# Beta, scatter halves and scatter order in the second attention stage of a two-layer kernel

## The chip, the cores and the metric

The kernel runs on one core of a Trainium2 chip, as one program. The metric is device time in microseconds of one execution. Three runs of the kernel before took 1773.91, 1776.12 and 1784.85 us; the median, 1776.12, stands for it. One more execution was profiled, and the rows below are from it.

## The reference

Two layers act on x, 64 x 64 tokens of 256 numbers (T = 4096 rows). Each layer is a cross attention and then a mixture of experts, both with a residual and a layer norm in front. What the change touches is in the second layer (and, for the scatter, in the first layer's experts too):

```python
x = x + _L0_xattn_ref(_layernorm(x), ctx, ...)
x = x + _L0_ffn_ref(_layernorm(x), ...)       # 16 experts, top 2, and a shared expert
x = x + _L1_xattn_ref(_layernorm(x), ctx, mask, ...)
x = x + _L1_ffn_ref(_layernorm(x), ...)       # 32 experts, top 4

# the end of _L1_xattn_ref
delta = rs * (ctx @ Wo.T + bo)
mu, var = delta.mean(-1), ((delta - mu) ** 2).mean(-1)
delta = (delta - mu) / sqrt(var + EPS_LN) * ln_gamma + ln_beta
# the routing of _L1_ffn_ref
topk_logits, topk_idx = top_k(x @ gate_w.T + gate_b, 4)
topk_weight = softmax(topk_logits)
y = sum over the 4 chosen experts of topk_weight * expert(x)
```

## The kernel before

The kernel is written by hand for the five engines; every wait is a semaphore written in the code, and each engine runs its own list of instructions in order. The 4096 rows are 32 tiles of 128 (NT); four tiles are a group (GT = 4, NG = 8). The stages follow one another: attention one (to 770 us of the span), the shared expert with the first routing (to 910), the experts of layer one (to 1050), attention two with the second routing (to 1425), the experts of layer two (to 1700), and a stage that adds the experts' rows up by token.

Attention two (`attention1`, line 1477) runs a software pipeline of steps r = 0, 1, 2, ... on each engine. In step r TensorE makes the scores of tile r + 1, the output of tile r and the projection of tile r - 1. VectorE's step (line 1903) clips the scores of tile r + 1, finishes the residual of tile r - 2 (`residual`, line 1892), normalises the heads of tile r and takes the mean and variance of the projected tile r - 1 (`delta_statistics`). At fixed places in a group's four steps it also does the layer norms in front of attention and experts (`norm_statistics` and `norm_apply`, lines 1437 to 1470: `apply_a` is the attention's, `apply_f` the experts') and the routing: `choose` picks four experts a token, `place_rows` gives each row its slot, `weigh` its weights.

GpSimd's step (line 1984) does for VectorE what VectorE hands it: `delta_deviation` (line 1978) raises the variance of tile r - 2 to the power -1/2; `add_beta` (line 1972) makes xb = x + beta for tile r - 1, which `residual` waits for; `deviation` (line 1969; the instruction is at 1456) does the power of a group's four variances. Early in the stage it also adds up the first layer's expert rows (lines 1964 and 1967). From step 10 on (FIRST) it runs one scatter round a step: `Routing.scatter` (line 1164) sends the four tiles of one group to the slots of their k-th expert. A round writes place (an integer) and weight into the tail of each row of xf, two copies, then issues four indirect DMAs of 128 rows of 1088 bytes. The same rows of xf are sent four times with different tails, so a round with k > 0 first waits until all four DMAs of the group's round before have landed (`scattered`). There are 32 rounds: the first 22 run in plain order (group by group, k = 0 to 3); the last ten are interleaved between groups 5, 6 and 7 by a list (lines 1573 to 1575):

```python
in_order = [(q, k) for q in range(NG) for k in range(m.K)][:NT - FIRST]
rounds = in_order + [(NG - 3, 2), (NG - 2, 0), (NG - 3, 3), (NG - 2, 1), (NG - 1, 0), (NG - 2, 2), (NG - 1, 1),
                     (NG - 2, 3), (NG - 1, 2), (NG - 1, 3)]
```

In step 33 GpSimd does the power of the last group (`last_group`) ahead of its scatter round. The four slot tables form a ring (RING = 4); `mark_sent` waits until a group's DMAs have all landed.

SyncE loads the second layer's weights into the room that attention two leaves, in 16 pieces of 512 KB (line 1609). Each load waits for a count of `tails_set`, so that the pieces go out with the last rounds, two a round; the last two wait for the round of index 29. After that SyncE writes the zero padding behind the experts' rows (`table_pads`, line 714; the DMAs are at line 726; ScalarE writes the other half), waits for all padding, and loads the first rows of the expert stage (lines 855 and 863), which also waits for GpSimd's last rounds to land.

The shared expert's stage calls the same `scatter` for its 16 rounds, with k = 0 and 1.

Of the kernel before, what the change touches and what calls it, by code (L numbers as in the profile page):

```python
# [4 lines left out]
F32 = mybir.dt.float32  # L5
BF16 = mybir.dt.bfloat16
I32 = mybir.dt.int32
# [4 lines left out]
P = 128  # L12
B, S, H = 64, 64, 256
T = B * S
NT = T // P
# [509 lines left out]
class Moe:  # L525
# [17 lines left out]
    def tables(self, ctx, nc, views=None):  # L543
# [5 lines left out]
        self.place = sbt("_place", [P, NG, K, GT], I32)  # L549
        self.weight = sbt("_weight", [P, NG, K, GT], F32)  # L550
# [22 lines left out]
class Constants:  # L573
# [6 lines left out]
    def tables(self, pool):  # L580
# [13 lines left out]
        for m in moes:  # L594
# [4 lines left out]
            nc.gpsimd.iota(m.place[:, :, :, :], pattern=[[GT * P * m.K, NG], [1, m.K], [P * m.K, GT]], base=0,  # L599
                           channel_multiplier=m.K).then_inc(made, 1)  # L600
            nc.gpsimd.memset(m.total[:, :], 0.0).then_inc(made, 1)
        nc.gpsimd.iota(sb["zeros"][:, DEST:DEST + 1].bitcast(I32), pattern=[[0, 1]], base=DUMP,
                       channel_multiplier=1).then_inc(made, 1)
# [177 lines left out]
def experts(stages, block, nc, sb, m, w_gu, w_down, bias, entered):  # L781
# [133 lines left out]
    def _(act):  # L915
# [3 lines left out]
        def step(it, r):  # L919
            if exists(it, r + 2):  # L920
# [4 lines left out]
                if q >= TAILS:  # L925
                    act.wait_ge(rows_stored[q % OUTS], 32 * ((q - TAILS) // OUTS + 1))
                nc.scalar.activation(dest[:, q % TAILS, :].bitcast(I32),
                                     rows[:, q % BODY, :, DEST].bitcast(I32), ACT.Copy)
# [94 lines left out]
class Routing:  # L1023
# [3 lines left out]
    def __init__(self, ph, nc, sb, m, wg, bias):  # L1027
# [24 lines left out]
        self.scattered = [ph.sem(f"scattered{n}") for n in range(Routing.RING)]  # L1052
# [64 lines left out]
    def weigh(self, dve, it, q, done):  # L1117
# [8 lines left out]
        nc.vector.tensor_tensor(m.weight[:, bass.ds(it * 2 + q, 1), :, :].rearrange("p a k j -> p (a j) k"), self.powers[:, :, :],  # L1126
# [37 lines left out]
    def scatter(self, pool, it, q, xn, k, turn, done):  # L1164

        m, nc = self.m, self.nc
        sent = 16 * GT
        slot, lap = (it * 2 + q) % self.RING, (it * 2 + q) // self.RING
        if k == 0:
            done(pool, self.slots_ready, it, q)  # L1170
            done(pool, self.weights_ready, it, q)
        else:
            pool.wait_ge(self.scattered[slot], lap * sent * m.K + sent * k)
        nc.gpsimd.tensor_copy(xn[:, :, DEST].bitcast(I32), m.place[:, it * 2 + q, k, :])
        nc.gpsimd.tensor_copy(xn[:, :, WEIGHT], m.weight[:, it * 2 + q, k, :]).then_inc(self.tails_set, 1)
        pool.wait_ge(self.tails_set, turn + 1)
        for j in range(GT):
            n = j * m.K + k
            pool.indirect_dma_start(m.rows_in, bass.IndirectOffsetOnAxis(ap=self.slots[:, slot, n:n + 1], axis=0),  # L1179
                                    xn[:, j, :], None).then_inc(self.scattered[slot], 16)  # L1180
# [5 lines left out]
    def mark_sent(self, pool, it, q):  # L1186

        n = 16 * GT * self.m.K
        slot, lap = (it * 2 + q) % self.RING, (it * 2 + q) // self.RING
        pool.wait_ge(self.scattered[slot], n * (lap + 1))  # L1190
# [1146 lines left out]
```

## Time and profile before

| | us |
|---|---|
| median of 3 runs (lowest, highest) | 1776.12 (1773.91, 1784.85) |
| the profiled execution, its own time | 1775.95 |
| its span in the profile | 1774.0 |
| busy in the span: TensorE, VectorE, ScalarE, GpSimd | 1533.0, 1332.5, 1094.1, 1093.0 |

The profile shows one execution: for each engine what instruction ran when, by the line of the kernel that issued it, how long the engine was idle before it and what ended that idle time. PE is TensorE, DVE is VectorE, ACT is ScalarE, POOL is GpSimd, SP is SyncE, and SPq is SyncE's queue. Times in rows are microseconds from the span's start, unless marked ns.

### The profile page before, as it was taken

To read this page: it belongs to the slowest core of one execution; us is meant where nothing else is said; L and a number is where in the kernel's file an instruction comes from. 1 tells how busy PE (TensorE), PEld (TensorE's weight loads), DVE (VectorE), ACT (ScalarE), POOL (GpSimd) and SP (SyncE) were. 2 spreads that over 40 slices of the span, in tenths; PEclk is the share of its full clock that TensorE was granted. 3 is DMA by queue.
4 is the path that set the end of the run, shared out by engine and by line. 5 is a ranking of instruction groups with operands and counts; after the bars stand their busy time and mean duration, and the time that the engine had idled before them with its cause. 6 is when DMAs were issued, how large, how long until landed. Compare 5 with 4: busy or idle time off the path is not lost.

```text
span 1774.0 us, 43982 instructions
## 1 busy us (share of the span) xinstructions
PE 1533.0 (86%) x14968; PEld 1236.6 (70%) x14968; DVE 1332.5 (75%) x2901; ACT 1094.1 (62%) x3516; POOL 1093.0 (62%) x1111
## 2 busy tenths in 40 slices
PE   6999999999999999989967755998895179999966
PEld 5888888888888888866646642565564179998955
DVE  6889899899999989876634344798886248887876
ACT  5888888888888888843335433656551056666610
POOL 4767667676666667647635554647776636666642
PEclk9999999999999999989989986999995589999988
DMA  8400000000000000022255424112213855554456
GB/s 230 128 20 20 20 20 20 20 20 20 12 19 20 20 20 20 8 97 84 79 176 155 151 80 161 49 38 94 83 71 113 311 167 165 162 158 150 125 200 275
DMA packets 103082, 167.66 MB, mean 95 GB/s; under 512 B 20224, under 2 KB 75981, under 8 KB 102481
## 3 DMA queue, kind: packets, MB, share of 16 engines
q1 hardware_dynamic: 73984, 103.46, 19.1%
q0 software_dynamic: 22272, 56.15, 8.6%
q10 hardware_dynamic: 6608, 5.25, 1.0%
q8 instruction: 124, 2.03, 0.5%
q14 instruction: 94, 0.76, 0.2%
HBM read 95.31 MB, written 75.76 MB: 96 GB/s over the span
## 4 chain that ended last, share of the span: by engine, by line
PE 68%; DVE 11%; issue 9%; POOL 3%; another core or an unknown queue 3%; ACT 2%; ACTq 1%; DMA 1%; SPq 1%; DVEq 0%; POOLq 0%
PE layers_banks L323 13%; PE layers_banks L294 13%; PE layers_banks L309 9%; PE layers_banks L890 9%; PE layers_banks L901 5%; PE layers_banks L1269 3%; PE layers_banks L277 3%; PE layers_banks L283 3%; PE layers_banks L878 2%; DVE weights L1862 2%; PE layers_banks L1282 1%; PE layers_banks L2152 1%; POOL l_rows_in L1179 1%; PE layers_banks L1071 1%
## 5 line engine op out<-in xcount | busy, mean ns | idle before, releaser
L468 POOL TENSOR_TENSOR w_down<-w_down,layers_arena 128x1024 f32<-128x1024 f32 x256 | 483.5, 1894 | 230.3 <-DVE layers_arena L424 229.3
L389 ACT ACTIVATE w_down<-layers_banks,layers_arena 128x256 f32<-128x256 f32 x1024 | 468.7, 498 | 2.8 <-DVE layers_arena L418 2.8
L1010 POOL DMA_INDIRECT l_by_token<-layers_arena x240 | 245.0, 1021 | 192.3 <-issue 104.2
L429 DVE COPY w_down<-layers_banks 128x1024 f32<-128x1024 f32 x256 | 312.2, 1220 | 40.4 <-PE layers_banks L309 36.2
L418 DVE TENSOR_REDUCE layers_arena<-layers_banks 128x4 f32<-128x1024 f32 x256 | 309.4, 1209 | 29.4 <-PE layers_banks L294 29.3
L294 PE MATMUL layers_banks<-layers_arena 64*128 64x256 f32 x2048 | 277.9, 383 | 3.7 <-ACT w_down L389 2.2
L323 PE MATMUL layers_banks<-w_down,layers_arena 128*64 128x256 f32 x2048 | 249.4, 385 | 1.7 <-DVE w_down L429 1.3
L389 ACT ACTIVATION_READ_ACCUMULATOR w_down<-layers_banks,layers_arena 128x1 f32 x1024 | 238.0, 232 | 0.0
L890 PE MATMUL layers_banks<-layers_arena 128*128 128x128 f32 x1600 | 204.1, 280 | 34.3 <-ACT layers_arena L933 30.7
L1179 POOL DMA_INDIRECT l_rows_in<-layers_arena,l_routing_group_slots x192 | 190.3, 991 | 57.7 <-issue 44.7
L309 PEld LDWEIGHTS layers_banks<-ident,w_down 64*128 64x128 f32 x4096 | 168.4, 138 | 77.5 <-issue 71.6
L890 PEld LDWEIGHTS layers_banks<-layers_arena 128*128 128x128 f32 x1600 | 192.3, 195 | 40.4 <-issue 40.0
L294 PEld LDWEIGHTS layers_banks<-layers_arena 64*128 64x128 f32 x2048 | 208.7, 188 | 6.0 <-issue 5.5
L309 PE MATMUL layers_banks<-ident,w_down 64*128 64x64 f32 x4096 | 178.7, 224 | 17.4 <-DVE w_down L429 3.4
L323 PEld LDWEIGHTS layers_banks<-w_down,layers_arena 128*64 128x64 f32 x2048 | 142.1, 136 | 61.5 <-DVE w_down L429 1.5
L986 DVE TENSOR_SCALAR layers_arena<-layers_banks,layers_arena 128x256 f32<-128x256 f32 x240 | 104.5, 477 | 75.5 <-PE layers_banks L901 41.0
L924 ACT ACTIVATE layers_arena<-layers_banks 128x512 f32<-128x512 f32 x120 | 70.5, 587 | 92.8 <-PE layers_banks L878 78.2
L353 ACT ACTIVATE layers_arena<-layers_banks 128x512 f32<-128x512 f32 x128 | 75.8, 592 | 82.0 <-PE layers_banks L283 82.0
L933 ACT ACTIVATE layers_arena<-weights 128x512 f32 (+1 forms) x240 | 119.6, 547 | 3.7 <-issue 3.7
L957 DVE TENSOR_SCALAR layers_arena<-layers_banks,l_block_bias 128x128 f32<-128x128 f32 x160 | 48.8, 346 | 87.1 <-PE layers_banks L890 84.7
L878 PE MATMUL layers_banks<-ident,layers_arena 128*128 128x128 f32 x480 | 75.4, 281 | 44.0 <-DMA layers_arena<-l_rows_in 44.0
L878 PEld LDWEIGHTS layers_banks<-ident,layers_arena 128*128 128x128 f32 x480 | 61.9, 146 | 57.0 <-issue 44.1
(227 smaller groups left out, 2552.3 us busy)
## 6 DMA issues: line engine op xcount, KB each, us to landing
layers_arena<-l_rows_in SPq DMA_DIRECT2D x240, 136.0 KB
weights<-l_by_token SPq DMA_DIRECT2D x32, 512.0 KB, 9.7
layers_arena<-in_ctx SPq DMA_DIRECT2D x64, 128.0 KB, 2.7
layers_arena<-l_by_token SPq DMA_DIRECT2D x32, 256.0 KB, 2.7
weights<-in_w_gu SPq DMA_DIRECT2D x16, 512.0 KB
l_rows_in<-zeros SPq DMA_DIRECT2D x1, 4352.0 KB
x_sb<-in_x SPq DMA_DIRECT2D x32, 128.0 KB, 2.5
w_down<-in_w_down SPq DMA_DIRECT2D x1, 4096.0 KB
```

The source lines that it names most:

```text
L294: last = nc.tensor.matmul(ps_s[:, b, 2 * h + qt, :], q_sb[half, p % 2, b, qt * P:(qt + 1) * P], ctx_d[half, p // TILE % 2, b, :], start=Tr ...
L309: last = nc.tensor.transpose(ps_t[:, d, kt, c * S:(c + 1) * S], prob[half, n % 4, c, kt * P:(kt + 1) * P], ident[half, half])
L323: last = nc.tensor.matmul(ps_qo[b * S:(b + 1) * S, 0, 0:A_N], vb[:, p // TILE % 2, kt, b, head * S:(head + 1) * S], prob_t[:, p % 2, b, kt ...
L389: last = nc.scalar.activation(prob[:, n % 4, c, :], ps_s[:, n % 2, c, :], ACT.Exp, bias=negmax[:, n % 2, c:c + 1], accum_out=sums[:, n % 2 ...
L418: nc.vector.tensor_reduce(negmax[:, n % 2, :], ps_s[:, n % 2, :, :], AX.X, ALU.max, negate=True).then_inc(max_ready, 1)
L429: nc.vector.tensor_copy(prob_t[:, n // 2 % 2, n % 2, :, :, :].rearrange("p k c (d s) -> p d (k c) s", d=2), ps_t[:, :, :, :].rearrange("p ...
L468: nc.gpsimd.tensor_tensor(prob[:, n % 4, :, :], prob[:, n % 4, :, :], rsum[:, n % 2, :].unsqueeze(2).to_broadcast([P, 4, A_N]), ALU.mult). ...
L878: last = nc.tensor.transpose(ps_x[:, q % 2, b, kt, :], rows[:, q % BODY, b, kt * P:(kt + 1) * P], sb["ident"][:, :])
L890: last = nc.tensor.matmul(ps_gu[:, q % 2, u, b, :], w_now[:, q % 2, b, kt, u * P:(u + 1) * P], rows_t[:, q % 2, b, kt, :], start=(kt == 0) ...
L933: last = nc.scalar.activation(w_now[:, r % 2, b, :, :].rearrange("p k n -> p (k n)"), w_gu[:, bass.ds(e[b], 1), :, :].rearrange("p a k n - ...
L1010: pool.indirect_dma_start(m.by_token, bass.IndirectOffsetOnAxis(ap=place, axis=0), outs[:, r % OUTS, b, :], None, bounds_check=T * m.K - 1 ...
L1179: pool.indirect_dma_start(m.rows_in, bass.IndirectOffsetOnAxis(ap=self.slots[:, slot, n:n + 1], axis=0), xn[:, j, :], None).then_inc(self. ...
```

## The change

Five things change. (1) `add_beta` goes from GpSimd to VectorE: `residual` makes xb itself, ahead of its wait for the power. (2) Place and weight lie side by side as two floats in one table, `tails`, instead of an integer table and a float table; what reads the place converts it to an integer. (3) A scatter round is two halves of two tiles: each half waits only for its own two DMAs of the group's round before, with a semaphore of its own, sets place and weight with one copy, and sends its two tiles. `tails_set` counts halves, and SyncE's thresholds double. (4) All 32 rounds run in plain order. (5) In step 33 the last group's power stands ahead of the fourth DMA of that step's round instead of ahead of the round.

```diff
-        self.place = sbt("_place", [P, NG, K, GT], I32)
-        self.weight = sbt("_weight", [P, NG, K, GT], F32)
+        self.tails = sbt("_tails", [P, NG, K, GT, 2], F32)
...
                 nc.scalar.activation(dest[:, q % TAILS, :].bitcast(I32),
-                                     rows[:, q % BODY, :, DEST].bitcast(I32), ACT.Copy)
+                                     rows[:, q % BODY, :, DEST], ACT.Copy)
...
-        self.scattered = [ph.sem(f"scattered{n}") for n in range(Routing.RING)]
+        self.scattered = [[ph.sem(f"scattered{n}_{half}") for half in range(2)] for n in range(Routing.RING)]
...
-    def scatter(self, pool, it, q, xn, k, turn, done):
+    def scatter(self, pool, it, q, xn, k, turn, done, ahead_of_last=None):
 
         m, nc = self.m, self.nc
-        sent = 16 * GT
+        sent = 16 * (GT // 2)
         slot, lap = (it * 2 + q) % self.RING, (it * 2 + q) // self.RING
         if k == 0:
             done(pool, self.slots_ready, it, q)
             done(pool, self.weights_ready, it, q)
-        else:
-            pool.wait_ge(self.scattered[slot], lap * sent * m.K + sent * k)
-        nc.gpsimd.tensor_copy(xn[:, :, DEST].bitcast(I32), m.place[:, it * 2 + q, k, :])
-        nc.gpsimd.tensor_copy(xn[:, :, WEIGHT], m.weight[:, it * 2 + q, k, :]).then_inc(self.tails_set, 1)
-        pool.wait_ge(self.tails_set, turn + 1)
-        for j in range(GT):
-            n = j * m.K + k
-            pool.indirect_dma_start(m.rows_in, bass.IndirectOffsetOnAxis(ap=self.slots[:, slot, n:n + 1], axis=0),
-                                    xn[:, j, :], None).then_inc(self.scattered[slot], 16)
+        for half in range(2):
+            tiles = slice(half * GT // 2, (half + 1) * GT // 2)
+            if k > 0:
+                pool.wait_ge(self.scattered[slot][half], lap * sent * m.K + sent * k)
+            nc.gpsimd.tensor_copy(xn[:, tiles, DEST:WEIGHT + 1], m.tails[:, it * 2 + q, k, tiles, :]).then_inc(self.tails_set, 1)
+            pool.wait_ge(self.tails_set, 2 * turn + half + 1)
+            for j in range(half * GT // 2, (half + 1) * GT // 2):
+                n = j * m.K + k
+                if j == GT - 1 and ahead_of_last is not None:
+                    ahead_of_last()
+                pool.indirect_dma_start(m.rows_in, bass.IndirectOffsetOnAxis(ap=self.slots[:, slot, n:n + 1], axis=0),
+                                        xn[:, j, :], None).then_inc(self.scattered[slot][half], 16)
...
-    in_order = [(q, k) for q in range(NG) for k in range(m.K)][:NT - FIRST]
-    rounds = in_order + [(NG - 3, 2), (NG - 2, 0), (NG - 3, 3), (NG - 2, 1), (NG - 1, 0), (NG - 2, 2), (NG - 1, 1),
-                         (NG - 2, 3), (NG - 1, 2), (NG - 1, 3)]
+    rounds = [(q, k) for q in range(NG) for k in range(m.K)]
+    IN_LOOP = NT - FIRST
...
-            sp.wait_ge(rt.tails_set, len(in_order) + 1 + n * (len(rounds) - len(in_order) - 2) // len(later))
+            sp.wait_ge(rt.tails_set, 2 * (IN_LOOP + 1 + n * (len(rounds) - IN_LOOP - 2) // len(later)))
...
         def residual(it, r):
             tile = x_sb[:, bass.ds(it * BODY + r, 1), :].rearrange("p a n -> p (a n)")
+            tdone(dve, x_ready, it, r - 1)
+            nc.vector.tensor_tensor(xb[:, r % 2, :], tile, w["beta"][:, :], ALU.add).then_inc(xb_ready, 1)
             tdone(dve, rstd_d_ready, it, r)
-            tdone(dve, xb_ready, it, r)
-            tdone(dve, x_ready, it, r - 1)
             nc.vector.scalar_tensor_tensor(out=scaled[:, :], in0=delta[:, r % 2, :], scalar=mv_d[:, r % 2, 0:1],
                                            in1=w["gamma"][:, :], op0=ALU.subtract, op1=ALU.mult).then_inc(scaled_ready, 1)
             tdone(dve, scaled_ready, it, r)
+            tdone(dve, xb_ready, it, r)
             nc.vector.scalar_tensor_tensor(out=tile, in0=scaled[:, :], scalar=rstd_d[:, r % 2:r % 2 + 1],
                                            in1=xb[:, r % 2, :], op0=ALU.mult, op1=ALU.add).then_inc(x_ready, 1)
...
-        def add_beta(it, r):
-            tdone(pool, scaled_ready, it, r - 2)
-            tdone(pool, x_ready, it, r - 2)
-            nc.gpsimd.tensor_tensor(xb[:, r % 2, :], x_sb[:, bass.ds(it * BODY + r, 1), :].rearrange("p a n -> p (a n)"),
-                                    w["beta"][:, :], ALU.add).then_inc(xb_ready, 1)
...
-            if texists(it, r - 1):
-                add_beta(it, r - 1)
...
             last_group = j == 1 and g == NG
+            ahead = None
             if last_group:
-                deviation(it, g - 1, vare_f, rstd_f, steps_f, xf_ready, rstd_f_ready)
+                def ahead():
+                    deviation(it, g - 1, vare_f, rstd_f, steps_f, xf_ready, rstd_f_ready)
             if 0 <= r - FIRST < len(rounds):
                 q, k = rounds[r - FIRST]
-                rt.scatter(pool, it, q, xf[:, q % XF, :, :], k, r - FIRST, gdone)
+                rt.scatter(pool, it, q, xf[:, q % XF, :, :], k, r - FIRST, gdone, ahead)
```

The parts left out fill `tails` and its readers in the same way (the iota of the places, the sigmoids and the weights of the routings, the last stage's weights) and wait for both halves in `mark_sent`.

## Rows read from the trace of the kernel before

**Rows 1.** Busy time by stretch: busy us (instructions) per engine, clock, DMA share.

```profile
core 0: us, PE busy (x) PEld busy (x) DVE busy (x) ACT busy (x) POOL busy (x), PEclk, DMA share, GB/s
770.00:910.00 140.00, 119.17 (x636) 79.67 (x632) 83.48 (x361) 42.87 (x76) 79.77 (x107) 0.95 0.30 111
1240.00:1273.00 33.00, 29.88 (x298) 19.59 (x296) 28.72 (x91) 19.28 (x33) 25.03 (x35) 1.00 0.26 86
1334.00:1368.00 34.00, 19.46 (x138) 14.48 (x136) 26.44 (x91) 4.70 (x7) 22.60 (x30) 0.50 0.28 97
1368.00:1426.00 58.00, 9.29 (x50) 7.14 (x50) 11.05 (x47) 1.24 (x2) 38.88 (x55) 0.50 0.83 290
```

**Rows 2.** Chain that ended last, in the loop: start us, us, what.

```profile
1240.56 1.31 DVE layers_arena L1441 x4
...
1266.19 1.40 another core or an unknown queue
...
1273.38 1.31 DVE layers_arena L1441 x4
```

**Rows 3.** Chain that ended last, at the stage's end, SyncE's part.

```profile
1403.90 0.33 SPq L1609
...
1423.26 1.93 DMA l_rows_in<-zeros
```

**Rows 4.** Timeline of GpSimd at the stage's end: start, us, then idle before and releaser.

```profile
1368.17 1.01 POOL L1456 TENSOR_TENSOR layers_arena<-layers_arena,minus_half 128x4 f32<-128x4 f32 x1 [4.21 <-DVE layers_arena L1449]
...
1387.27 0.19 POOL L1174 COPY layers_arena<-l_place 128x4 int32<-128x4 int32 x1 [1.70 <-DVE l_weight L1126]
...
1392.78 0.21 POOL L1174 COPY layers_arena<-l_place 128x4 int32<-128x4 int32 x1
1392.90 0.20 POOL L1175 COPY layers_arena<-l_weight 128x4 f32<-128x4 f32 x1
1393.38 0.98 POOL L1179 DMA_INDIRECT l_rows_in<-layers_arena,l_routing_group_slots  x1 [0.28 <-issue]
...
1398.16 0.20 POOL L1174 COPY layers_arena<-l_place 128x4 int32<-128x4 int32 x1
...
1416.89 0.19 POOL L1174 COPY layers_arena<-l_place 128x4 int32<-128x4 int32 x1 [2.58 <-DMA l_rows_in<-layers_arena,l_routing_group_slots]
...
1421.29 0.96 POOL L1179 DMA_INDIRECT l_rows_in<-layers_arena,l_routing_group_slots  x1 [0.30 <-issue]
```

**Rows 5.** Groups of GpSimd, 1060 to 1430: busy us, mean ns, idle before.

```profile
L1975 POOL TENSOR_TENSOR layers_arena<-x_sb,w_beta 128x256 f32<-128x256 f32 x32 | 23.9, 747 | 0.0
...
L1174 POOL COPY layers_arena<-l_place 128x4 int32<-128x4 int32 x32 | 8.4, 261 | 14.1 <-DMA l_rows_in<-layers_arena,l_routing_group_slots 12.3 <-DVE l_weight L1126 1.7
```

**Rows 6.** Timeline of VectorE, two independent adds one after the other.

```profile
1062.42 0.42 DVE L1848 TENSOR_TENSOR x_sb<-x_sb,layers_arena 128x256 f32<-128x256 f32 x1
1062.77 0.42 DVE L1846 TENSOR_TENSOR layers_arena<-layers_arena 128x256 f32<-128x256 f32 x1
```

**Rows 7.** Timeline of VectorE: residual and apply instructions, stretched and not.

```profile
1141.67 0.94 DVE L1897 SCALAR_TENSOR_TENSOR layers_arena<-layers_arena,w_gamma 128x256 f32<-128x256 f32 x1 [2.81 <-POOL layers_arena L1981]
...
1214.33 0.48 DVE L1897 SCALAR_TENSOR_TENSOR layers_arena<-layers_arena,w_gamma 128x256 f32<-128x256 f32 x1
...
1215.88 1.42 DVE L1465 TENSOR_SCALAR layers_arena<-x_sb,layers_arena 128x256 f32<-128x256 f32 x4
...
1218.95 1.79 DVE L1465 TENSOR_SCALAR layers_arena<-x_sb,layers_arena 128x256 f32<-128x256 f32 x4 [0.17 <-POOL layers_arena L1456]
```

**Rows 8.** Timeline of VectorE: its waits in steps 26, 27 and 31.

```profile
1314.87 0.42 DVE L1880 TENSOR_TENSOR layers_arena<-layers_banks,w_bo 128x256 f32<-128x256 f32 x1 [0.76 <-PE layers_banks L1687]
...
1317.81 1.23 DVE L1862 TENSOR_SCALAR weights<-layers_banks 128x1024 f32<-128x1024 f32 x1 [1.37 <-PE layers_banks L1650]
...
1349.51 0.95 DVE L1897 SCALAR_TENSOR_TENSOR layers_arena<-layers_arena,w_gamma 128x256 f32<-128x256 f32 x1 [1.91 <-issue]
```

**Rows 9.** Timeline of GpSimd: three of the beta adds.

```profile
1126.34 0.73 POOL L1975 TENSOR_TENSOR layers_arena<-x_sb,w_beta 128x256 f32<-128x256 f32 x1
...
1133.75 0.72 POOL L1975 TENSOR_TENSOR layers_arena<-x_sb,w_beta 128x256 f32<-128x256 f32 x1
...
1219.40 0.87 POOL L1975 TENSOR_TENSOR layers_arena<-x_sb,w_beta 128x256 f32<-128x256 f32 x1
```

**Rows 10.** Groups of the page: one of ScalarE in the expert stages.

```profile
L924 ACT ACTIVATE layers_arena<-layers_banks 128x512 f32<-128x512 f32 x120 | 70.5, 587 | 92.8 <-PE layers_banks L878 78.2
```

More of the change, by code:

```diff
@@ L598, in tables @@
                            allow_small_or_imprecise_dtypes=True).then_inc(made, 1)
-            nc.gpsimd.iota(m.place[:, :, :, :], pattern=[[GT * P * m.K, NG], [1, m.K], [P * m.K, GT]], base=0,
-                           channel_multiplier=m.K).then_inc(made, 1)
+            nc.gpsimd.iota(m.tails[:, :, :, :, 0], pattern=[[GT * P * m.K, NG], [1, m.K], [P * m.K, GT]], base=0,
+                           channel_multiplier=m.K, allow_small_or_imprecise_dtypes=True).then_inc(made, 1)
             nc.gpsimd.memset(m.total[:, :], 0.0).then_inc(made, 1)
-        nc.gpsimd.iota(sb["zeros"][:, DEST:DEST + 1].bitcast(I32), pattern=[[0, 1]], base=DUMP,
-                       channel_multiplier=1).then_inc(made, 1)
+        nc.gpsimd.iota(sb["zeros"][:, DEST:DEST + 1], pattern=[[0, 1]], base=DUMP,
+                       channel_multiplier=1, allow_small_or_imprecise_dtypes=True).then_inc(made, 1)
     def tables_made(self, eng):
@@ L1125, in weigh @@
         dve.sem_inc(self.passed, 1)
-        nc.vector.tensor_tensor(m.weight[:, bass.ds(it * 2 + q, 1), :, :].rearrange("p a k j -> p (a j) k"), self.powers[:, :, :],
+        nc.vector.tensor_tensor(m.tails[:, it * 2 + q, :, :, 1].rearrange("p k j -> p j k"), self.powers[:, :, :],
                                 self.share[:, 1, :].unsqueeze(2).to_broadcast([P, GT, m.K]), ALU.mult)\
@@ L1186, in mark_sent @@
     def mark_sent(self, pool, it, q):
-        n = 16 * GT * self.m.K
+        n = 16 * (GT // 2) * self.m.K
         slot, lap = (it * 2 + q) % self.RING, (it * 2 + q) // self.RING
-        pool.wait_ge(self.scattered[slot], n * (lap + 1))
+        for half in range(2):
+            pool.wait_ge(self.scattered[slot][half], n * (lap + 1))
         pool.sem_inc(self.rows_sent, 1)
@@ L1335, in sigmoids @@
             done(act, rt.behind_ready, it, q)
-            nc.scalar.activation(m.weight[:, bass.ds(it * 2 + q, 1), 0, :], rt.behind[:, :, 1].unsqueeze(1), ACT.Sigmoid,
+            nc.scalar.activation(m.tails[:, it * 2 + q, 0, :, 1], rt.behind[:, :, 1], ACT.Sigmoid,
                                  scale=-1.0)
-            nc.scalar.activation(m.weight[:, bass.ds(it * 2 + q, 1), 1, :], rt.behind[:, :, 1].unsqueeze(1), ACT.Sigmoid)\
+            nc.scalar.activation(m.tails[:, it * 2 + q, 1, :, 1], rt.behind[:, :, 1], ACT.Sigmoid)\
                 .then_inc(rt.weights_ready, 1)
@@ L2180, in expert_weights @@
             nc.vector.tensor_tensor(weighted[:, :, :, :], onehot[:, :, :, :],
-                                    m.weight[:, g, :, :].rearrange("p k j -> p j k").unsqueeze(3)
+                                    m.tails[:, g, :, :, 1].rearrange("p k j -> p j k").unsqueeze(3)
                                     .to_broadcast([P, GT, K, E]), ALU.mult).then_inc(expert_steps, 1)
```

## The prediction

> **What bounds the kernel now.** I read the page's chain and groups first, then the busy times by stretch, then the chain and the timelines of VectorE, GpSimd and SyncE inside attention two. All edits but the scatter's own lie in attention two, 1060 to 1425 us of the span. The stretches [rows 1] show TensorE 29.9 and VectorE 28.7 us busy of 33 in the middle of its loop, and TensorE 19.5 of 34, at half clock, at its end; from 1368 on only GpSimd, issuing indirect DMAs, and the DMA engines are busy. In the loop the chain of waits is VectorE nearly throughout: four tiles take 1273.38 - 1240.56 = 32.8 us, broken by waits on "another core or an unknown queue" [rows 2]. There are four such between 1150 and 1308, 1.4 to 1.8 us each; the row shows the third. TensorE, just behind, is the second limit. GpSimd keeps pace; what it does shows only where VectorE waits for it.
>
> The end is another matter. After VectorE's last statistics GpSimd runs nine scatter rounds, and SyncE may issue the last weight loads only when the round of index 29 has its tails set; it then writes 16 blocks of padding, the last of which ends the stage [rows 3]. Two chains therefore end almost together: GpSimd's last DMA issue ends at 1421.29 + 0.96 = 1422.3 [rows 4] and still has to land, and SyncE's padding lands at 1425.2 [rows 3]. SyncE's is the later.
>
> **Beta on VectorE.** GpSimd loses 32 adds of 0.75 us [rows 5]; VectorE gets 32 of 128x256 f32 from SBUF. A like add takes 0.42, but the next independent one starts 1062.77 - 1062.42 = 0.35 later [rows 6]; in residual() nothing depends on the add until after the next instruction, so I take 0.35 a tile. The bounds: 0 where VectorE would have waited anyhow; at most 0.35 + (0.94 - 0.48) = 0.81, if the add is stretched as L1897 is where a GpSimd tensor op runs beside it [rows 7]. I stay with 0.35, since GpSimd's tensor op of that size is the one that goes.
>
> The Trainium skill, "VectorE: DVE Perf Modes", section on the DRAIN, says that the next instruction does not start until the pipe is empty. That would make the add cost its whole 0.42, and the sum 1.5 us more; the rows show 0.35.
>
> Which of the 32 lie on the path? Tiles 0 to 3: VectorE waits for GpSimd or TensorE there (2.8 us at tile 3 [rows 7]), so hidden. Tiles 25 and 26: it waits 0.76 and 1.37 for TensorE [rows 8], hidden. Tile 29: it waits 1.91 for GpSimd's power, behind a scatter round [rows 8], hidden. That leaves 25. Four of these stand right before the waits on an unknown queue [rows 2], whose end VectorE does not set, so they are swallowed. So 21 x 0.35 = +7.4 us.
>
> Taken off: from 1118 to 1141 the chain is GpSimd itself, adding up expert rows, with two beta adds of 0.7 between them [rows 9]: -1.4. L1897 at 1141.67 would also get back 0.46, but the two new VectorE adds there run beside GpSimd's tensor ops and stretch those; I let these cancel. In five groups the four instructions of apply_a take 1.79 instead of 1.42, each time with a beta add beside them (the row at 1219.40 stands inside the one at 1218.95) [rows 7, 9]: 5 x 0.37 = -1.9. The loop thus gives 7.4 - 1.4 - 1.9 = +4.1: the last statistics come 4.1 us later.
>
> **Half rounds.** A round now takes 1398.16 - 1392.78 = 5.38, of which 0.60 pass before its first DMA [rows 4]; the four DMAs and three gaps of 0.30 are 4.78. One copy instead of two saves 0.12 before the first DMA, and a second copy and wait, 0.48, takes the place of one gap of 0.30: 4.78 - 0.30 + 2 x 0.48 = 5.44. So half rounds cost +0.06 each, but a half waits only for its own two DMAs of the round before, with 2.7 us of the other half between. In the loop the landing waits are 12.3 us in all [rows 5], hidden behind VectorE; removing them brings nothing. The shared expert also runs scatter(), but TensorE has 119 busy of 140 us there [rows 1] and is its chain: 0. Place as a float, read by ScalarE with a conversion, and weights at stride two keep the number of instructions and of elements; in the expert stage ScalarE sits 92.8 us idle before L924 alone [rows 10]: 0, and if 240 such small copies grew by a tenth of a microsecond, still under that cover.
>
> **Plain order and the power between.** Before, GpSimd is idle 4.2 us before the last group's power at 1368.17, 1.7 before group 7's first round and 2.6 for a landing before the last one [rows 4]. After, three DMAs of round 23 fill the first idle time; then come the power (1.0), one DMA, and eight rounds: 1368.2 + 1.0 + 1.0 + 8 x 5.44 = 1413.7, before the shift of 4.1. Group 7's first round would begin at 1370.2 + 4 x 5.44 = 1392, after its weights (1387.3), so the 1.7 goes. GpSimd's chain gains 8.5.
>
> SyncE's does not. Its gate is the second half of round 29: 1370.2 + 5 x 5.44 + 2.9 = 1400.3, against 1403.9 [rows 3]: -3.6 at best. Rounds 28 to 31 are now all of group 7, in the stretch where the DMA engines are 83% busy [rows 1], and I must bound the landing: 2.6 us after the last issue (the wait at 1416.89) as the lower end; as the upper, 5.4, since the round at 1398.16 does not wait for the one whose DMAs ended at 1392.78 [rows 4]. Two halves hide 2.7, so round 29 waits 0 to 2.7 and the gate gains 3.6 to 0.9. I take the middle, -2.3; what SyncE does after the gate, 21.3 us, stays. The later GpSimd rounds, with up to three such waits, end at 1413.7 to 1421.8 and stay about level with SyncE.
>
> Sum: +4.1 - 2.3 = +1.8 us. Against the profiled execution, 1775.95 us (span 1774.0 and 1.95 around it), that is 1777.8; the median of the three runs is 0.2 higher: 1778.
>
> **Rivals.**
> - *The adds are free*: VectorE's new 0.35 vanishes in TensorE's time. For: TensorE is almost as full, and the waits on an unknown queue [rows 2] are not VectorE's. Against: between 1150 and 1200 VectorE waits for nobody. Then -1.4 - 1.9 - 2.3 = -5.6: 1770.5.
> - *The padding is not the end*: with the loads issued earlier, SyncE's padding finds its queue empty and GpSimd's -8.5 counts in full: 4.1 - 8.5 = -4.4, 1771.7. Against: the loads move with the rounds, so the padding meets the same queue.
> - *The added operand blocks*: slower. Each new add, with two inputs in SBUF, is stretched by 0.46 as L1897 was, and 21 x 0.81 = 17.0 instead of 7.4: +11.4, 1787.5. For: that row [rows 7]. Against: L1897 at 1214.33 takes 0.48 while an indirect DMA is being issued. It decides from 0.27 us a tile, where the adds eat all three gains (5.6/21). The Trainium skill, "SBUF — State Buffer", section "SBUF: two separate sides", has this rule: a VectorE instruction with two SBUF inputs and a GpSimd instruction that reads SBUF exclude each other for the whole instruction. The trace agrees for L1897 beside L1975; for the small tail copies no row shows it.
> - *The clock falls in the loop*: TensorE, waiting more, drops to half clock before 1334, as it does there now. One group at half clock adds about 29.9 us of TensorE time less 3 us of slack: 1805. Against: full clock in the loop's stretches [rows 1].
>
> **How the numbers follow.** The forecast 0.50, free adds 0.20, padding 0.10, blocked adds 0.12, clock 0.05, something else 0.03. The landing bounds move the forecast by 1.4 either way, the runs themselves by several. From 1770.5 less that spread to 1787.5 plus it gives 1767 to 1789. One per cent, 17.8 us, is about what can be told from no change: faster than 1758 only by something unseen, 0.03; slower than 1794 by the clock or a mishap, 0.06; within, 0.91.
>
> **What would show it.** Right: 32 new VectorE adds of about 0.42; four tiles of the loop in about 34 us; the 1.79 of apply_a back at 1.42; no GpSimd idle time before the last power; landing waits near 3 us instead of 12; 21 us between SyncE's last load and the first expert rows. Wrong: four tiles still in 32.8, or new adds of 0.8, or padding that ends well after or before GpSimd's last landing.

## The result, and the profile after

The changed kernel took 1806.37 us (median of 4 runs, 1801.14 to 1810.43) against 1775.17 us for the kernel before (4 runs beside it). The ratio of their runs is 1.0146, with a 95% interval from 1.0115 to 1.0177. The two medians are 31.2 us apart; by the ratio the change costs about 26 us. The forecast was 1778, +1.8, with 1767 to 1789 as its range. The profiled execution of the changed kernel took 1801.14 us with a span of 1799.3, so the two profiled executions are 25.3 us apart in their spans.

Where these 25.3 us lie follows from the starts of a few instructions in both traces: the first routing logits of the shared expert's stage, the experts' first row load (SyncE), the first `add_parts` and the first and last clip of attention two (VectorE), the last logits (TensorE), and the row loads again.

| stretch, us | before | after | difference |
|---|---|---|---|
| to the first logits | 783.9 | 782.2 | -1.7 |
| shared expert: first logits to first row load | 124.9 | 141.8 | **+16.9** |
| first experts, to the first add_parts | 153.2 | 152.3 | -0.9 |
| to the first clip | 38.4 | 38.4 | 0 |
| attention two's loop: first to last clip | 241.5 | 254.0 | **+12.5** |
| last clip to last logits | 35.1 | 36.3 | +1.2 |
| tail: last logits to first row load | 49.0 | 48.3 | -0.7 |
| first to last row load of the second experts | 244.8 | 241.9 | -2.9 |
| the rest | 103.2 | 104.1 | +0.9 |

Two stretches hold the loss: one in which the forecast had 0, and one in which it had +4.1. Stretches with the same code differ between executions: the shared stage of kernels that do not touch it lies between 124 and 128.5, the second experts' between 240 and 251, and two kernels below with the same loop (e4 and e7) have it at 243.4 and 238.1. A difference of 5 us between two loops, each from one execution, is therefore not told from none; the two losses above are well beyond that.

**The shared expert's stage.** Busy times of the whole stretch, after and then before; the columns are those of [rows 1].

```profile
782.00:924.00 142.00, 122.68 (x560) 78.64 (x560) 73.26 (x333) 41.31 (x71) 76.58 (x103) 0.90 0.27 102
```

```profile
784.00:909.00 125.00, 111.99 (x560) 74.86 (x560) 73.51 (x333) 40.95 (x70) 74.20 (x102) 0.96 0.30 113
```

TensorE runs the same 560 matmuls, 10.7 us longer busy at a lower granted clock; VectorE does no more than before, GpSimd 2.4 us more. The group of TensorE that grew is the gate and up product. After, then before (busy us, mean ns of one, idle before it):

```profile
L1272 PE MATMUL layers_banks<-layers_arena,weights 128*128 128x512 f32 x128 | 69.0, 699 | 11.8 <-DVE x_sb L1396 8.2 <-issue 3.7
```

```profile
L1269 PE MATMUL layers_banks<-layers_arena,weights 128*128 128x512 f32 x128 | 58.4, 607 | 4.4 <-DVE x_sb L1393 3.6 <-issue 0.7
```

Busy +10.6 and idle +7.4 make 18.0, no less than the whole stretch's 16.9. One group shows how. TensorE before: down product, gate and up of the next group, down again.

```profile
828.59 3.63 PE L1282 MATMUL layers_banks<-weights,layers_arena 128*128 128x256 f32 x16
...
833.28 7.11 PE L1269 MATMUL layers_banks<-layers_arena,weights 128*128 128x512 f32 x16 [0.73 <-DVE x_sb L1393]
...
842.83 3.63 PE L1282 MATMUL layers_banks<-weights,layers_arena 128*128 128x256 f32 x16
```

VectorE before, the residual that follows the down product: the first pair of tiles needs its first eight matmuls, the second pair the other eight.

```profile
830.71 0.86 DVE L1393 SCALAR_TENSOR_TENSOR x_sb<-layers_banks,layers_arena,x_sb 128x256 f32<-128x256 f32 x2
832.25 0.88 DVE L1393 SCALAR_TENSOR_TENSOR x_sb<-layers_banks,layers_arena,x_sb 128x256 f32<-128x256 f32 x2 [0.68 <-PE layers_banks L1282]
```

TensorE after, and VectorE after:

```profile
848.41 3.63 PE L1285 MATMUL layers_banks<-weights,layers_arena 128*128 128x256 f32 x16
...
854.45 8.80 PE L1272 MATMUL layers_banks<-layers_arena,weights 128*128 128x512 f32 x16 [2.08 <-DVE x_sb L1396]
...
865.70 3.63 PE L1285 MATMUL layers_banks<-weights,layers_arena 128*128 128x256 f32 x16
```

```profile
852.64 1.66 DVE L1396 SCALAR_TENSOR_TENSOR x_sb<-layers_banks,layers_arena,x_sb 128x256 f32<-128x256 f32 x4 [2.35 <-remote]
```

The down product takes 3.63 us in both. Before, VectorE starts on the first pair 2.1 us after its beginning. After, it starts 4.2 us after it, and then does all four tiles at once. "remote" means that a semaphore moved at that moment, but no instruction in the profile ends near it: by the record of its rows TensorE was through with these eight matmuls some 2.3 us earlier. I call this a late handover. The next gate and up product, which needs the same bank, begins 854.45 - 848.41 = 6.04 us after the down product instead of 4.69 (+1.35), and takes 8.80 instead of 7.11 (+1.69), since TensorE, after 2.08 us idle, is granted half its clock (0.50, the 1.2 GHz level) soon after it has resumed:

```profile
854.00:856.00 2.00, 1.55 (x3) 0.82 (x4) 1.85 (x9) 0.00 (x0) 0.00 (x0) 0.82 0.00 0
856.00:858.00 2.00, 2.00 (x3) 0.67 (x2) 1.86 (x12) 0.00 (x0) 1.38 (x2) 0.50 0.00 0
```

Together 3.04 us a group: the period is 17.29 (865.70 - 848.41) instead of 14.24 (842.83 - 828.59). On GpSimd the difference is the landing wait, which is there before (first fence) and gone after (second):

```profile
845.62 0.19 POOL L1174 COPY layers_arena<-weights 128x4 int32<-128x4 int32 x1 [2.93 <-DMA l_rows_in<-layers_arena,l_routing_group_slots]
```

```profile
846.03 0.19 POOL L1175 COPY layers_arena<-weights 128x4 f32<-128x4 f32 x1
```

**The loop.** VectorE's waits over 20 tiles in the middle, before and after:

```profile
DVE layers_arena L1082 <- remote: 3.6, 2, 1.8
DVE weights L1862 <- remote: 2.5, 2, 1.2
DVE layers_arena L1880 <- PE layers_banks L1687: 0.8, 1, 0.8
```

```profile
DVE layers_arena L1871 <- remote: 11.7, 9, 2.2
DVE weights L1864 <- PE layers_banks L1652: 2.6, 4, 1.0
DVE layers_arena L1081 <- remote: 1.4, 2, 0.7
```

```profile
1168.90:1342.60 173.70, 151.42 (x1449) 98.24 (x1446) 142.97 (x453) 93.73 (x154) 97.14 (x132) 0.96 0.20 68
```

The last row is the same 20 tiles after, 173.7 us; before they took 161.0 with VectorE 138.45 busy:

```profile
1156.80:1317.80 161.00, 144.62 (x1437) 94.82 (x1436) 138.45 (x433) 92.71 (x154) 109.95 (x151) 1.00 0.22 74
```

Of the +12.7, VectorE's work is 4.5, late handovers 13.1 - 6.1 = 7.0. Most are now at L1871, where VectorE takes up TensorE's product of weights and values (I call it P·V). VectorE's new adds are as forecast from [rows 6], and the apply instructions are no longer stretched as in [rows 7]:

```profile
L1468 DVE TENSOR_SCALAR layers_arena<-x_sb,layers_arena 128x256 f32<-128x256 f32 x37 | 13.0, 412 | 0.0
...
L1897 DVE TENSOR_TENSOR layers_arena<-x_sb,w_beta 128x256 f32<-128x256 f32 x20 | 8.4, 419 | 0.0
```

**The tail.** GpSimd's landing waits at the end, from 1395 on, where before the row at 1416.89 in [rows 4] had the only long one; and SyncE's timeline, whose end answers to [rows 3]:

```profile
POOL layers_arena L1175 <- DMA l_rows_in<-layers_arena,l_routing_group_slots: 8.0, 5, 2.9
```

```profile
1384.94 51.36 SPq L1611 DMA_DIRECT2D weights<-in_w_gu  x16
1437.03 12.07 SPq L725 DMA_DIRECT2D l_rows_in<-zeros  x16
```

SyncE's last padding is issued by 1449.1. GpSimd's last scatter issue runs to 1450.59, and the row loads start at 1453.3. So GpSimd's chain, not SyncE's, now ends the stage.

### The profile page after: what moved, and what is told of

Read it like the earlier page. It is cut to its first block and busy times, and to the rows that moved or that the text cites. A ratio compares the mean times of both kernels' runs of the same rounds, so it can differ in the third digit from the quotient of the medians.

```text
span 1799.3 us, 43952 instructions
## 1 busy us (share of the span) xinstructions
PE 1552.0 (86%) x14968; PEld 1248.4 (69%) x14968; DVE 1340.5 (74%) x2933; ACT 1094.4 (61%) x3516; POOL 1078.0 (60%) x1079
## 5 line engine op out<-in xcount | busy, mean ns | idle before, releaser
L889 PE MATMUL layers_banks<-layers_arena 128*128 128x128 f32 x1600 | 208.2, 283 | 28.4 <-ACT layers_arena L932 23.4
## 6 DMA issues: line engine op xcount, KB each, us to landing
layers_arena<-in_ctx SPq DMA_DIRECT2D x64, 128.0 KB, 2.7
x_sb<-in_x SPq DMA_DIRECT2D x32, 128.0 KB, 2.5
```

Source lines behind the costliest of these rows:

```text
L889: last = nc.tensor.matmul(ps_gu[:, q % 2, u, b, :], w_now[:, q % 2, b, kt, u * P:(u + 1) * P], rows_t[:, q % 2, b, kt, :], start=(kt == 0) ...
```

## The experiments

Times stand as medians with the ratio to the kernel before on the same chip; the lengths of stretches are each from one profiled execution, by the marks of the table above.

**Landing waits put back, in both scatter stages** (e1):

```diff
+        if k > 0:
+            for half in range(2):
+                pool.wait_ge(self.scattered[slot][half], lap * sent * m.K + sent * k)
         for half in range(2):
             tiles = slice(half * GT // 2, (half + 1) * GT // 2)
-            if k > 0:
-                pool.wait_ge(self.scattered[slot][half], lap * sent * m.K + sent * k)
```

> The changed kernel with one thing put back, in both scatter stages: a round with k > 0 waits for all four DMAs of the group's round before at its top, and only then sends its two halves. Theory A (the landing wait was useful: without it GpSimd issues eight indirect DMAs with no pause, and the signals of TensorE then arrive late): the shared expert's stage, first logits to the experts' first row load, falls from 141.7 us to 124 to 128, the loop of attention two, first to last clip, from 254.1 to 244 to 249, and the whole time to 1778 to 1788. Theory B (the half-size copies, the new table or the doubled semaphores slow the stage, not the missing wait): the shared stage stays at 140 or above and the whole at 1798 to 1808.

Measured: 1810.91 us, ratio 1.0155 (1.0112 to 1.0198). Shared stage 125.4, loop 251.6, tail 64.3 instead of 48.3. In the shared stage theory A holds: 16.4 us come back though the half-size copies, the new table and the doubled semaphores are all still there. The loop keeps most of its loss (251.6, outside the 244 to 249 of theory A), and the whole time was mispredicted, because whole waits and plain order do not go together in the tail: GpSimd waits 19.4 us for landings there.

```profile
POOL layers_arena L1176 <- DMA l_rows_in<-layers_arena,l_routing_group_slots: 19.4, 5, 5.2
```

**Landing waits put back in the shared stage alone** (e2): the same edit under `m.K == 2`.

> As e1_whole_wait, but the whole-round wait stands only in the shared expert's stage; attention two keeps its waits by half. Theory A: shared stage 124 to 128, loop of attention two 252 to 256 as in the changed kernel, whole time 1786 to 1793. Theory B: shared stage 140 or above, whole 1798 to 1808. If the loop's extra time comes from the beta adds alone, e1_whole_wait and this run show the same loop; if the missing landing wait has a part in it, this one's loop is 5 us or more the longer.

Measured: 1790.34 us, ratio 1.0051 (1.0026 to 1.0077). Shared stage 124.3, loop 255.7, tail 48.0. TensorE's gate and up product is back to 58.1 us busy and 4.4 idle, and GpSimd waits for landings again:

```profile
L1275 PE MATMUL layers_banks<-layers_arena,weights 128*128 128x512 f32 x128 | 58.1, 604 | 4.4 <-DVE x_sb L1399 4.4
```

```profile
POOL layers_arena L1178 <- DMA l_rows_in<-layers_arena,l_routing_group_slots: 13.6, 8, 2.3
```

So 13.6 us of waiting on GpSimd save 17 us of the stage. The whole times say the same: 1.0051 instead of 1.0146 is some 17 us. The loop is 4.1 us longer than in e1, just short of the 5 named: the landing waits have at most a small part in its loss.

**Beta on VectorE alone** (e3): the kernel before with the new `residual` and without `add_beta`.

> The kernel before with one part of the change alone: the 32 beta adds on VectorE. The step under test is the forecast's +4.1 us for the loop of attention two, which was 241.5 us. Theory A (the adds cost as the forecast had it, the rest of the loop's loss is late signals): loop 243 to 248, whole time 1776 to 1781. Theory C (nothing hides the adds: 32 times 0.35 to 0.42 us): loop 252 to 255, whole 1785 to 1789. The shared expert's stage stays at 124.8 by either.

Measured: 1794.12 us, ratio 1.0062 (1.0033 to 1.0091). Loop 257.4, +15.9, against 32 x 0.42 = 13.4 by theory C; one execution does not tell these apart. The waits do: over 20 tiles, 17.2 us longer than before, VectorE is 4.6 us more busy and waits 19.8 us for "remote" instead of 6.1, so its adds are not the whole of it.

**Beta back on GpSimd** (e4): the changed kernel with the old `add_beta` and `residual`.

> The changed kernel with the beta adds back on GpSimd; half rounds, plain order and the rest stay. Theory A: the loop of attention two, 254.1 us, keeps the loss that comes from the scatter's missing landing waits and loses only the adds: 248 to 251; shared stage 141 as in the changed kernel; whole time 1796 to 1803. Theory C (the loop's whole loss is the adds): loop 241 to 243, whole 1788 to 1793.

Measured: 1795.79 us, ratio 1.009 (1.0048 to 1.0132). Loop 243.4, shared stage 141.4. The loop is cured by undoing the beta part, with half rounds in place. By the numbers this is theory C; the waits in e3 speak against its reason. A third theory, D, was formed: the loss comes from GpSimd's side of the move. Without its add of 0.75 us GpSimd begins each scatter round sooner, and the round then overlaps TensorE's handovers.

**No add at all** (e5): the kernel before, without `add_beta`, `residual` reading x.

```diff
-                                           in1=xb[:, r % 2, :], op0=ALU.mult, op1=ALU.add).then_inc(x_ready, 1)
+                                           in1=tile, op0=ALU.mult, op1=ALU.add).then_inc(x_ready, 1)
```

> The kernel before without the 32 beta adds on any engine; the residual takes x in place of x + beta, so that the addition of beta is left out of the output. GpSimd has then the free time of the changed kernel and VectorE no more to do than before. Theory D (the loop of attention two loses because GpSimd, rid of the add, issues its DMAs earlier against TensorE's work, so that TensorE's signals come late; VectorE's own 0.35 to 0.42 us a tile are the smaller part): loop 246 to 253 against 241.5 before, though work was only taken away, and whole time 1778 to 1788. Theory C (VectorE's adds are the cost): loop 236 to 241.5, whole 1768 to 1776.

Measured: 1787.39 us, ratio 1.0045 (1.0012 to 1.0079). Loop 252.7: **11.2 us longer with work only taken away**. Theory D's number; C falls. By the interval of the whole time the loss is 2 to 14 us. VectorE is 135.81 us busy over 20 tiles, less than before, and waits:

```profile
1159.50:1332.60 173.10, 149.20 (x1445) 96.36 (x1442) 135.81 (x433) 93.67 (x154) 95.67 (x131) 0.98 0.20 68
```

```profile
DVE layers_arena L1869 <- remote: 15.5, 8, 3.9
DVE weights L1862 <- remote: 2.0, 1, 2.0
```

One of these handovers: TensorE's P·V, the round on GpSimd, and VectorE's instruction that waits for P·V.

```profile
1219.82 1.13 PE L1679 MATMUL layers_banks<-layers_arena,weights 128*64 128x34 f32 x32
```

```profile
1217.95 1.06 POOL L1179 DMA_INDIRECT l_rows_in<-layers_arena,l_routing_group_slots  x1 [0.29 <-POOL layers_arena L1175]
...
1221.85 0.96 POOL L1179 DMA_INDIRECT l_rows_in<-layers_arena,l_routing_group_slots  x1 [0.30 <-DVE x_sb L1899]
```

```profile
1223.78 0.26 DVE L1869 RECIPROCAL layers_arena<-layers_banks 128x16 f32<-128x16 f32 x1 [2.20 <-remote]
```

P·V ends at 1220.95 by its row, in the midst of the round's four DMAs, and VectorE gets it at 1223.78.

**The add on both engines** (e6): as e3, but GpSimd still makes an add of the same size at the old place, into a tile that nobody reads.

> The kernel before with the beta add on VectorE, as in e3_before_beta_dve, and an add of the same size (gamma + beta, into a tile that nobody reads) still on GpSimd at the old place. Theory D: GpSimd's DMAs keep their old time against TensorE's work, so the loop loses only VectorE's own part of about 4 to 8 us, 245 to 250, and the whole is 1778 to 1785. Theory C: the loop is as long as in e3_before_beta_dve, 253 to 259, or longer since the two adds now also run beside each other, and the whole is 1787 to 1797.

Measured: 1784.59 us, ratio 1.0035 (1.0007 to 1.0063). Loop 243.2, 14.2 less than e3: a useless add on GpSimd takes the loss away. The whole times of e3, e5 and e6 have intervals that overlap, so this rests on the loops of single executions; over all fourteen kernels these fall into two groups, 238.1 to 243.4 and 251.6 to 257.4. The loop is 243.2 - 241.5 = 1.7 us longer than before, less than theory D had. That is not the price of VectorE's adds: over 20 tiles VectorE is 144.47 us busy instead of 138.45, 6.0 more, and waits 2.1 instead of 6.1 for "remote", 4.0 less, so that 2.0 are left.

```profile
DVE weights L1863 <- remote: 2.1, 3, 1.0
```

**Whole waits in the shared stage and beta on GpSimd** (e7): e2 and e4 in one, half rounds and plain order kept in attention two.

> The changed kernel with the two losing parts put back: whole-round landing waits in the shared expert's stage, beta on GpSimd. Half rounds, plain order and the power between them stay in attention two. If the losses add up as the runs so far say: shared stage 124 to 126, loop 242 to 245, tail from the last logits to the experts' first row load 48 to 49, and the whole 1771 to 1778, no better than the kernel before by more than 5 us.

Measured: 1776.76 us, ratio 0.9976 (0.9945 to 1.0007); shared stage 128.0, loop 238.1, tail 48.4. The two losses do add up, in the whole times too: 0.51% is left in e2, 0.90% in e4, 1.46% in the changed kernel and nothing that can be told in e7. It is the best of all versions tried, but not told from the kernel before.

**A pause in place of the landing wait** (e8): the changed kernel, with four adds into a spare tile between the two rounds of a group in the shared stage.

> The changed kernel, with half waits everywhere, but in the shared expert's stage GpSimd does four adds into a spare tile, about 3 us in all, between the two rounds of a group, in place of the landing wait of 2 to 3 us that the kernel before has there. Theory A1 (what helps is the pause between the rounds' DMAs): shared stage 124 to 128 us and no wait of VectorE's L1396 for a late signal. Theory A2 (what helps is that the first round has landed before the next is issued, or the adds themselves disturb VectorE): shared stage 135 or more.

Measured: 1799.13 us, ratio 1.0124 (1.0092 to 1.0156). Shared stage 130.7; L1398 waits once, 1.3 us, for "remote", where the changed kernel waits 11.7 us. Between the two ranges and nearer to A1: in this execution a pause does most of it without a landing. The adds cost something by themselves, for VectorE now waits 20.1 us in the stage for GpSimd's power, against 6.9 before. But the profiled execution, 1790.24 us, is the fastest of eight, and the whole times do not tell e8 from the changed kernel (1.0124 and 1.0146, with intervals that overlap). So that a pause is enough, and that what has landed matters little, is likely and not shown.

**The spare add behind the round** (e9): e6 with the add moved behind the scatter call of its step.

> As e6_before_both_add (loop 243.2), but GpSimd's spare add stands behind its scatter round instead of ahead of it, so that GpSimd is as busy and the round's first DMA is issued 0.75 us sooner after the power. Theory D1 (what counts is when the round's DMAs start against TensorE's step): loop 250 to 258, as without the add, whole time 1786 to 1796. Theory D2 (what counts is that GpSimd has less room between rounds): loop 242 to 246, whole 1779 to 1786.

Measured: 1789.88 us, ratio 1.0109 (1.0075 to 1.0143). Loop 256.9. GpSimd is as busy as in e6, and the loss is back: what counts is when the round begins, not how much GpSimd does (D1). The whole times agree, as far as two chips can be compared: the intervals of e6 and e9 do not overlap.

```profile
DVE layers_arena L1870 <- remote: 8.1, 5, 2.9
DVE layers_arena L1082 <- remote: 3.1, 2, 1.6
```

**Two spare adds ahead of the round** (e10):

> As e6_before_both_add, but with two spare adds of 0.7 us ahead of each round instead of one. Theory D1: another 0.7 us moves the rounds against TensorE's step once more; signals that came late in e6_before_both_add, mostly those 3 to 5 us behind a round's first DMA, move or not, and the loop is anything from 238 to 256, but differs from 243 by over 3 us. Theory D2: more work between the rounds is as good or better, 240 to 244, as long as GpSimd keeps pace.

Measured: 1789.27 us, ratio 1.011 (1.0071 to 1.015). Loop 255.1, yet with hardly a late handover; this run does not tell D1 from D2. GpSimd is now the trouble in the plain way: its power comes late, and its adds stretch VectorE's apply to 552 ns (464 in e6).

```profile
DVE layers_arena L1465 <- POOL layers_arena L1456: 3.4, 4, 1.1
...
DVE layers_arena L1870 <- remote: 0.9, 1, 0.9
```

```profile
L1465 DVE TENSOR_SCALAR layers_arena<-x_sb,layers_arena 128x256 f32<-128x256 f32 x37 | 18.2, 552 | 3.4 <-POOL layers_arena L1456 3.4
```

**Half rounds in the old order** (e11): e7 with the old list of the last ten rounds and the power ahead of its step's round.

> As e7_half_tail_beta_pool (shared stage with whole waits, beta on GpSimd, half rounds in attention two; tail 48.4 us from the last logits to the experts' first row load), but the last ten rounds in the old interleaved order and the last group's power ahead of its step's round, as before. If the plain order only moves landing waits about, as its 8.0 us of waits in the tail say: tail 44 to 47, better than with plain order, and whole time 1770 to 1776. If plain order and the power between them bring what the forecast said: tail 50 to 52, whole 1777 to 1781.

Measured: 1772.77 us, ratio 1.0005 (0.9989 to 1.0021). Tail 47.4 against 48.4 with plain order: between both expectations, and a difference of 1.0 that one execution does not tell. GpSimd waits less for landings there (the first fence is e11, the second e7), but it gains nothing that shows in the whole.

```profile
POOL layers_arena L1178 <- DMA l_rows_in<-layers_arena,l_routing_group_slots: 2.5, 1, 2.5
```

```profile
POOL layers_arena L1178 <- DMA l_rows_in<-layers_arena,l_routing_group_slots: 7.2, 3, 3.0
```

**All five edits, both causes taken away** (e12): e2 with e6's spare add on GpSimd.

> The changed kernel with all five edits, but the two supposed causes of its loss taken away: whole-round landing waits in the shared expert's stage (as in e2_whole_wait_shared, loop 255.7), and an add of beta's size on GpSimd ahead of each scatter round of attention two, into a tile that nobody reads. If the two causes are the whole loss: shared stage 124 to 128, loop 241 to 247, whole time within 8 us of the kernel before on the same chip. If the adds on VectorE cost by themselves in the presence of half rounds: loop 250 or more, whole 12 us or more above the kernel before.

Measured: 1773.62 us, ratio 1.0013 (0.9993 to 1.0034). Shared stage 124.1, loop 241.6, tail 48.2. With 32 adds more on VectorE and 32 useless ones on GpSimd the kernel is as fast as before, and no wait for "remote" is among VectorE's longest over 20 tiles. The two causes are the whole loss, to within what the interval leaves (-1 to +6 us).

```profile
1155.60:1315.80 160.20, 144.03 (x1439) 94.52 (x1436) 144.22 (x454) 93.24 (x154) 112.00 (x151) 1.00 0.22 73
```

The traces of all these kernels give one more count. Over the same 20 tiles I took the end of each P·V (start plus length of its row) and the start of the first indirect DMA of the round then under way, and counted the P·V that end over 0.6 us behind that start, while the round's DMAs are still being issued. The limit of 0.6 was chosen with the traces in sight:

| kernel | P·V inside a round, of 20 | 20 tiles, us |
|---|---|---|
| e7 | 0 | 157.5 |
| e12 | 0 | 160.2 |
| e4 | 2 | 160.8 |
| before | 1 | 161.0 |
| e11 | 5 | 161.7 |
| e6 | 0 | 163.0 |
| e1 | 12 | 171.2 |
| e10 | 1 | 172.3 |
| e5 | 13 | 173.1 |
| after | 16 | 173.7 |
| e9 | 9 | 174.4 |
| e2 | 16 | 175.3 |
| e8 | 16 | 175.4 |
| e3 | 12 | 178.2 |

The kernels of 163 us or less have at most five, mostly two or fewer; the others have 9 or more, but for e10, where GpSimd was late for another reason. The count is a sign and no price: e11's VectorE waits 8.1 us behind its five, and its 20 tiles are as short as before.

## Why the prediction was wrong, point by point

**"The shared expert also runs scatter() ... and is its chain: 0."** This step failed, by 16.9 us, and was the larger miss. That TensorE is the chain there was right; that GpSimd's waits could therefore go without a price was not. The 14.5 us of landing waits on GpSimd were a pause in the DMA issue. Without it TensorE's results reach VectorE up to 2.7 us late, TensorE then idles 2 us a group and goes on at half clock. e2 shows that the missing wait alone is the cause; that it works as a pause is what e8 makes likely.

**"GpSimd loses 32 adds", and "So 21 x 0.35 = +7.4 us".** The rows were right: an add took 0.419 us, and the apply instructions came back from 472 to 412 ns, 37 of them from 15.3 to 13.0 us, -2.3 where the forecast had -1.9. The sign of being right, four tiles in about 34 us, came true too (173.7 / 5 = 34.7), but by luck: 7.0 of the 12.7 us over 20 tiles are late handovers. With GpSimd's add kept, the loop is 1.7 us longer in e6 than before, and 3.5 longer in e12 than in e7 (241.6 and 238.1); both are less than the forecast's 7.4 and within what one execution tells. That does not make the adds free: in e6 they are 6.0 us of VectorE's time over 20 tiles, most of it offset by fewer late handovers, on which the forecast had no term. What was missing is a term for GpSimd's side: the sentence "what it does shows only where VectorE waits for it" left out when it issues its DMAs. Taking its add away cost 11.2 us by itself (e5), more than everything that the forecast weighed for the loop. The waits on "another core or an unknown queue" [rows 2] were the sign. I used them as a cover that swallows four adds and did not ask what they were: handovers that came late, the very thing that the change multiplied.

**"Half rounds cost +0.06 each."** As forecast in size: in the tail a round without waits goes from the copy at 1398.22 to that at 1403.67, 5.45 us. The 12.3 us of landing waits that it put into the loop are those up to 1430 [rows 5]: 9.7 lie in the loop, the rest is the row at 1416.89. That removing them "brings nothing" in the loop held; that it costs nothing held there too, as far as e1 and e2 tell (4 us between them).

**"SyncE's ... I take the middle, -2.3."** The tail gained 0.7. The bound of the landings was too low: 0 to 2.7 us were allowed before round 29, while the five waits of the tail make 8.0, four of them (6.3 us) up to round 29's tails. SyncE's last load went out by 1436.3 and the row loads came 17 us later, not 21, because GpSimd's chain had become the end: from the last power to the end of the last issue 1450.59 - 1395.92 = 54.7 us, against 54.1 before and at most 53.6 in the forecast. The idle time before that power did not go either: 1.40 us were left of the 4.2 in [rows 4]. Half rounds do make the plain order bearable: with whole waits the tail is 64.3 (e1). But only the plain order needs them for that; with half rounds and the old order (e11) the tail is 47.4, not longer than with the plain one.

**"Place as a float ... 0."** Nothing in the expert stages speaks against it: 152.3 us for the first after 153.2.

**The rivals.** Blocked operands did not decide anything: an add took 0.419 us over the 20 tiles, though only three of these adds ran beside a tail copy. Two early ones, beside GpSimd's adding of expert rows, took 0.69 and 0.68, as the forecast expected there. The clock did fall, but mostly in the shared stage (0.96 to 0.90), which the rival did not name; over the 20 tiles of the loop it went from 1.00 to 0.96, with TensorE 6.8 us longer busy and not 27. Its 1805 was near the result by accident.

Sum of the misses: 16.9 in the shared stage, 12.5 - 4.1 = 8.4 in the loop, 1.6 in the tail, -3.4 in stretches with no edit of weight: 23.5, against 1801.14 - 1777.8 = 23.3.

## What to carry to other kernels

An engine that only waits is not free to run earlier: where GpSimd issues indirect DMAs, ask which of TensorE's results fall into the issue of a round, before taking work or a wait out in front of it. To see whether a moved operation costs on the engine that receives it or on the one that loses it, run it on neither and on both; here the loop was 11.2 us longer in the first case and 1.7, no more than executions differ, in the second. And a wait that the profile puts down to no known instruction deserves a look before it is used as cover.

## What the runs showed of the hardware

Results of TensorE reach the other engines late while GpSimd's indirect DMAs are being issued: 2.20 us of waiting behind P·V in the row at 1223.78, 2.35 us behind the down product in the row at 852.64, while in the first row of VectorE shown of the shared stage before, at 830.71, there is no wait at all. The effect hangs on the time within a round: in the kernel before and in e4, P·V that ended between rounds, or within half a microsecond of the start of the round's first DMA, kept VectorE waiting for 0.5 us at most, and the kernels where it often falls later are the long ones of the table.

The Trainium skill, "Perfetto Trace Analysis", section "Tensor Engine Instruction (MATMUL, LD_WEIGHTS)", says that the profile's end of a matmul is worked out from its size, and that the signal goes out only after the written bytes have been acknowledged. The trace agrees in that the end of the row and the handover can lie 2.3 us apart.

What holds the handover back is not settled: the matmuls may end later than the rows say, or their signals may be on the way. The rows of e5 around 1223.78 speak for the signals:

```profile
1220.88 1.98 PE L1629 MATMUL layers_banks<-weights,w_k 128*128 128x512 f32 x4
1222.69 1.03 PE L1687 MATMUL layers_banks<-w_o,layers_arena 128*128 128x256 f32 x4
```

```profile
1223.84 0.69 ACT L1755 ACTIVATE weights<-layers_banks,w_bk 128x512 f32<-128x512 f32 x1 [0.87 <-PE layers_banks L1629]
```

TensorE goes on behind P·V with two more groups of matmuls. ScalarE waits for the first of them, whose row ends at 1222.86, 1.9 us after that of P·V, yet it starts within 0.06 us of VectorE: results that TensorE finished one after the other arrive together, 1.0 us after the round's last issue has ended (1221.85 + 0.96 = 1222.81). As the ends of matmuls are worked out, this is no proof. No run was made in which the scatter's DMAs go through another engine, so that it is their issue on GpSimd and not their traffic that counts is not shown either.
